# Double steps in the attention and feed-forward turns of a decoder block: two score tiles an instruction, whole outputs

## What is computed

```
x = x + attn(layernorm(x))                       # 16 heads, not touched
# cross-attention: q = layernorm(x), k = v = ctx; rows are split in 8 heads of 64 rows
qk  = einsum('bhdq,bhdl->bhql', qh, kh) / sqrt(64)
ret = einsum('bhql,bhdl->bhdq', softmax(qk), vh)
x = x + gamma * ret
# feed-forward, hidden size 1365, ternary weights w1q, w3q, w2q
g = silu(layernorm(x) @ w1q.T) * (layernorm(x) @ w3q.T)
x = x + g @ w2q.T
```

## Time and profile before

| | us |
|---|---|
| median of three runs | 1113.23 (1113.21 to 1115.01) |
| profiled execution | 1114.2 |
| its span, first to last instruction | 1112.1 |
| PE, DVE, ACT, POOL busy | 1104.1, 731.4, 550.5, 483.9 |
| turn (1, 0) | about 723 to 831 |
| turn (2, 1) | about 831.7 to 939 |
| turn (3, 2) | about 939 to 1047 |
| last turn, with the output's write | about 1047 to 1112 |

### The profile page before, as it was taken

The page is one execution under the profiler, slowest core; times in us unless marked ns, Lnnn a source line. Parts: engine busy times, 40 slices in busy tenths (PEclk is TensorE's granted clock), DMA queues, the critical chain, the costliest instruction groups (busy, mean ns, idle before and its releaser), DMA issues.

```text
span 1112.1 us, 15909 instructions
## 1 busy us (share of the span) xinstructions
PE 1104.1 (99%) x5840; PEld 938.7 (84%) x5840; DVE 731.4 (66%) x1347; ACT 550.5 (50%) x1149; POOL 483.9 (44%) x430
## 2 busy tenths in 40 slices
PE   9999999999999999999999999999999999999998
PEld 8888888878888888888888888888888888888886
DVE  7555547787777688866424334689967976887531
ACT  4556673324243376667515233167627763775130
POOL 1322327341424275665344040157728762875130
PEclk9999999999999999999999999999999999999999
DMA  7455553544533724212631112362113211310101
GB/s 246 164 189 189 185 176 129 171 126 159 173 111 93 230 96 142 86 39 86 252 114 38 38 59 65 140 205 63 53 52 101 77 49 58 113 49 1 38 1 38
DMA packets 54663, 122.20 MB, mean 110 GB/s; under 512 B 10057, under 2 KB 10057, under 8 KB 52538
## 3 DMA queue, kind: packets, MB, share of 16 engines
q1 hardware_dynamic: 54586, 121.18, 33.3%
HBM read 103.32 MB, written 17.84 MB: 109 GB/s over the span
## 4 chain that ended last, share of the span: by engine, by line
PE 94%; DVE 2%; DMA 1%; ACT 1%; issue 1%; POOL 0%; SPq 0%; POOLq 0%; DVEq 0%
PE bank L176 19%; PE bank L178 19%; PE bank L177 19%; PE bank L583 7%; PE bank L584 7%; PE bank L541 5%; PE bank L599 4%; PE bank L598 4%; PE bank L565 3%; PE bank L566 3%; PE bank L551 2%; PE bank L552 2%; DMA x1d<-x_scratch 1%; PE bank L608 0%; DVE x3l L860 0%
## 5 line engine op out<-in xcount | busy, mean ns | idle before, releaser
L583 PE MATMUL bank<-x3h,w 128*128 128x512 f32 (+2 forms) x368 | 143.5, 393 | 0.4 <-DVE x3l L860 0.3
L1471 ACT ACTIVATE yh<-bank 128x512 fp32r<-128x512 f32 x64 | 38.1, 600 | 209.9 <-PE bank L178 209.8
L584 PE MATMUL bank<-x3l,w 128*128 128x512 f32 (+2 forms) x368 | 140.6, 385 | 0.0
L940 POOL TENSOR_SCALAR pe_x<-pe_x,xri,gam 128x512 f32<-128x512 f32 x96 | 76.2, 795 | 78.5 <-DVE xri L779 76.1
L775 DVE TENSOR_REDUCE xmx<-bank 128x1 f32<-128x512 f32 x128 | 87.7, 687 | 32.9 <-PE bank L552 31.4
L2143 POOL TENSOR_TENSOR wal<-raw_a,wah 128x512 fp32r<-128x512 f32 x44 | 61.0, 1413 | 109.5 <-ACT wah L1513 109.5
L176 PE MATMUL bank<-wah,gh 128*128 128x512 f32 x256 | 102.6, 401 | 0.0
L2148 POOL TENSOR_TENSOR wbl<-raw_b,wbh 128x512 fp32r<-128x512 f32 x64 | 87.0, 1383 | 34.1 <-ACT wbh L1534 33.8
L176 PE MATMUL bank<-yh,rh 128*128 128x512 f32 x256 | 100.4, 392 | 0.8 <-DVE xacc L1979 0.8
L176 PE MATMUL bank<-wah,ph 128*128 128x512 f32 x256 | 100.1, 391 | 0.0
L177 PE MATMUL bank<-wal,gh 128*128 128x512 f32 x256 | 100.1, 391 | 0.0
(11 more groups left out here) (181 smaller groups left out, 3014.7 us busy)
## 6 DMA issues: line engine op xcount, KB each, us to landing
raw_a<-in_wk SPq DMA_DIRECT2D x8, 1024.0 KB, 5.2
raw_b<-in_wq SPq DMA_DIRECT2D x8, 1024.0 KB, 5.6
raw_a<-in_wo SPq DMA_DIRECT2D x8, 1024.0 KB, 5.1
raw_b<-in_wvt SPq DMA_DIRECT2D x8, 1024.0 KB, 5.0
ternary_scratch<-wraw SPq DMA_DIRECT2D x24, 341.2 KB, 3.0
x1d<-x_scratch SPq DMA_DIRECT2D x48, 128.0 KB, 3.1
kd<-in_ctx SPq DMA_DIRECT2D x48, 128.0 KB, 3.0
w<-ternary_scratch SPq DMA_DIRECT2D x2, 2730.0 KB, 11.1
```

The lines of the kernel that those rows point to most:

```text
L583: pe.matmul(u_bank[w][0:m, cols], lhs, x3h[:, c, cols], start=c == 0, stop=False)
L584: mm = pe.matmul(u_bank[w][0:m, cols], lhs, x3l[:, c, cols], start=False, stop=c == CK - 1)
L940: pool.tensor_scalar(m.pe_x[:, q, :], m.pe_x[:, q, :], xri[:, q:q + 1], gam[:], ALU.mult, ALU.mult).then_inc(s["xpn"], 1)
```

## The change

A turn has 16 double steps (`STEPS`), each for two score tiles (h, q) and (h, q + 1) with q = 0 or 2.

- The first four banks are two PSUM tensors of two banks each, so that one instruction can read two tiles: maxima (`dve_max_two`), reciprocals, the high and low parts of the transposed shares (`act_px_two`, `dve_px_two`). Exponentials and shares stay one tile an instruction.
- PE makes two score tiles, then two transposed tiles, then in steps q = 0 a whole output with 512 columns (`pe_ret_whole`) of head h - 2, then one up piece, or two in the odd steps from 3 to 13.
- ACT, steps q = 0: both exponentials, then a wait for the output of head h - 2, then the high parts; steps q = 2: the high parts, then the exponentials. Keys and queries come behind the gate.
- DVE: maxima, reciprocals of the step before, an up product, the next head's queries, `dve_ret`, the low parts, a further up product.
- POOL: the next head's queries first, then shares, the up part, keys, values.
- The rest of head 7 stands otherwise between the down tiles; four matmuls of down tile 1 move ahead of the last output.
- `r_done` gives the count of the semaphore r_ready, as sequence 0 still makes halves.

```diff
-        bank = [stack.enter_context(nc.psum_tensor(f"bank{i}", [P, 512], F32)) for i in range(8)]
+        two = [stack.enter_context(nc.psum_tensor(f"two{i}", [P, 2, 512], F32)) for i in range(2)]
+        bank = [t[:, k] for t in two for k in range(2)]
+        bank += [stack.enter_context(nc.psum_tensor(f"bank{i}", [P, 512], F32))[:] for i in range(4, 8)]
...
+        STEPS = 2 * XH
...
-            if n < 0 or n >= S_TILES:
+            if n < 0 or n >= STEPS:
                 return range(0)
-            return range(U_PIECES * n // S_TILES, U_PIECES * (n + 1) // S_TILES)
+            first = n + max(0, min(n, STEPS - 2) // 2 - 1)
+            return range(first, first + (2 if n % 2 and 1 < n < STEPS - 1 else 1))
...
+        def pe_ret_whole(pe, m, b, h):
+            pe.wait_ge(s["t_free"], t_p(b, h, 3) + 1)
+            if h % 2 == 0:
+                pe.wait_ge(s["vtl"], b * V_TILES + h // 2 + 1)
+            pe_wait(pe, "r_free", b * XH + h, 1)
+            for c in range(CK):
+                lhs = m.vts[:, h % 4, c, :]
+                pe.matmul(m.r[:], lhs, m.pxh[:, c, :], start=c == 0, stop=False)
+                mm = pe.matmul(m.r[:], lhs, m.pxl[:, c, :], start=False, stop=c == CK - 1)
+            mm.then_inc(s["r_ready"], 1)
...
         def pe_turn(pe, b, f, nxt):
+            for n in range(STEPS):
+                h, q = n // 2, n % 2 * 2
+                if b is not None:
+                    for k in (q, q + 1):
+                        pe_sx(pe, main, b, h, k)
+                    if h:
+                        for k in (q, q + 1):
+                            pe_pt(pe, main, b, h - 1, k)
+                    if h >= 2 and q == 0:
+                        pe_ret_whole(pe, main, b, h - 2)
+                if f is not None:
+                    for piece in pieces(n):
+                        pe_up(pe, f, piece)
             if f is not None:
                 pe_down(pe, f, 0, range(0, HC // 2))
             if b is not None:
-                pe_pt(pe, main, b, XH - 1, 2)
+                pe_ret_whole(pe, main, b, XH - 2)
+                pe_pt(pe, main, b, XH - 1, 0)
+                pe_pt(pe, main, b, XH - 1, 1)
             if f is not None:
                 pe_down(pe, f, 0, range(HC // 2, HC))
             if b is not None:
+                pe_pt(pe, main, b, XH - 1, 2)
                 pe_pt(pe, main, b, XH - 1, 3)
-                pe_ret(pe, main, b, XH - 1, 0)
             if f is not None:
-                pe_down(pe, f, 1, range(0, 3))
+                pe_down(pe, f, 1, range(0, HC // 2))
             if b is not None:
-                pe_ret(pe, main, b, XH - 1, 1)
+                pe_ret_whole(pe, main, b, XH - 1)
             if f is not None:
-                pe_down(pe, f, 1, range(3, HC))
+                pe_down(pe, f, 1, range(HC // 2, HC))
...
+        def act_px_two(act, b, h, q):
+            tiles, high, _ = shares(h, q)
+            act.wait_ge(s["t_ready"], t_p(b, h, q + 1) + 1)
+            act.activation(high, tiles, ACT.Copy).then_inc(s["pxh"], 2)
...
         def act_turn(act, b, f, nxt):
+            for n in range(STEPS):
+                h, q = n // 2, n % 2 * 2
                 if f is not None:
+                    for piece in pieces(n - 1)[-1:]:
                         act_tanh(act, f, piece)
                 if b is not None:
+                    if h and q:
+                        act_px_two(act, b, h - 1, q)
+                    elif h:
+                        act.wait_ge(s["t_ready"], t_p(b, h - 1, q + 1) + 1)
                     act_exp(act, main, b, h, q)
+                if f is not None:
+                    for piece in pieces(n)[:-1]:
+                        act_tanh(act, f, piece)
+                if b is not None:
+                    act_exp(act, main, b, h, q + 1)
+                    if h >= 2 and q == 0:
+                        act.wait_ge(s["r_ready"], r_done(b, h - 2))
+                    if h and q == 0:
+                        act_px_two(act, b, h - 1, q)
+                if f is not None:
+                    for piece in pieces(n - 1):
+                        act_gate(act, f, piece)
+                if b is not None:
                     if prep_step(h) == n:
+                        act_prep(act, main, b, h + 1)
+                    if h % 2 == 0 and values_step(h) == n:
+                        act_vt(act, main, b, h)
...
+        def dve_px_two(dve, b, h, q):
+            tiles, high, low = shares(h, q)
+            dve.wait_ge(s["pxh"], b * S_TILES + (4 * h + q + 2))
+            dve.tensor_tensor(low, tiles, high.bitcast(F32), ALU.subtract).then_inc(s["t_free"], 2)
+
+        def dve_max_two(dve, b, h, q):
+            dve.wait_ge(s["s_ready"], b * S_TILES + (4 * h + q + 2))
+            dve.reduce_max(xmx[:, q:q + 2], two[0][:], axis=AX, negate=True).then_inc(s["xmx"], 2)
...
         def dve_turn(dve, b, f, nxt, between=None):
+            for n in range(STEPS):
+                h, q = n // 2, n % 2 * 2
                 if b is not None:
+                    dve_max_two(dve, b, h, q)
+                    if n:
+                        dve_rinv_two(dve, b, (n - 1) // 2, (n - 1) % 2 * 2)
                 if f is not None:
+                    for piece in pieces(n - 1)[-1:]:
                         dve_up(dve, f, piece)
                 if b is not None:
                     if prep_step(h) == n:
                         dve_q(dve, main, b, h + 1)
+                    if q == 0 and h >= 2:
+                        dve_ret(dve, main, b, h - 2)
+                    if h:
+                        dve_px_two(dve, b, h - 1, q)
+                if f is not None:
+                    for piece in pieces(n)[:-1]:
+                        dve_up(dve, f, piece)
...
         def pool_turn(pool, b, f, nxt):
+            for n in range(STEPS):
+                h, q = n // 2, n % 2 * 2
+                if b is not None and prep_step(h) == n - 1:
+                    pool_queries(pool, main, b, h + 1)
+                if b is not None and n:
+                    for k in range(2):
+                        pool_prob(pool, main, b, (n - 1) // 2, (n - 1) % 2 * 2 + k)
...
                 if b is not None:
+                    if prep_step(h) == n:
+                        pool_keys(pool, main, b, h + 1)
                     if n - 1 in map(values_step, range(0, XH, 2)):
+                        pool_vt(pool, main, b, h)
```

More of the change, by code:

```diff
@@ L48 @@
 assert WP * WS * GROUPS == HID * C
-TANH_LAG, GATE_LAG = 1, 1
 WARM = 34
@@ L693, in act_px, with shares @@
             act.activation(m.pxh[:, :, q * P:(q + 1) * P], tb, ACT.Copy).then_inc(s["pxh"], 1)
+        def shares(h, q):
+            cols = slice(q * P, (q + 2) * P)
+            return (two[1][:].rearrange("p k (c n) -> p k c n", n=P),
+                    pxh[:, :, cols].rearrange("p c (k n) -> p k c n", n=P),
+                    pxl[:, :, cols].rearrange("p c (k n) -> p k c n", n=P))
+        def act_px_two(act, b, h, q):
+            tiles, high, _ = shares(h, q)
+            act.wait_ge(s["t_ready"], t_p(b, h, q + 1) + 1)
+            act.activation(high, tiles, ACT.Copy).then_inc(s["pxh"], 2)
         def act_exp(act, m, b, h, q):
@@ L730, in act_turn @@
                     act_exp(act, main, b, h, q)
-                    if prep_step(h) == n:
[L732 to L739, removed]
@@ new lines, in act_turn @@
+                if f is not None:
+                    for piece in pieces(n - 1):
+                        act_gate(act, f, piece)
+                if b is not None:
+                    if prep_step(h) == n:
+                        act_prep(act, main, b, h + 1)
+                    if h % 2 == 0 and values_step(h) == n:
+                        act_vt(act, main, b, h)
+            if f is not None:
+                for piece in pieces(STEPS - 1)[-1:]:
+                    act_tanh(act, f, piece)
+                for piece in pieces(STEPS - 1):
+                    act_gate(act, f, piece)
@@ L746, in act_turn @@
             if b is not None:
-                for q in range(4):
-                    act_px(act, main, b, XH - 1, q)
+                for q in (0, 2):
+                    act_px_two(act, b, XH - 1, q)
                 if nxt is not None:
@@ L870, in dve_turn @@
                 if f is not None:
-                    for piece in pieces(n - TANH_LAG):
+                    for piece in pieces(n - 1)[-1:]:
                         dve_up(dve, f, piece)
                 if b is not None:
-                    if h:
-                        dve_px(dve, main, b, h - 1, q)
-                    if n:
-                        dve_rinv(dve, main, b, (n - 1) // 4, (n - 1) % 4)
                     if prep_step(h) == n:
                         dve_q(dve, main, b, h + 1)
-                    if q == 3 and h >= 4 and h % 2 == 0:
+                    if q == 0 and h >= 2:
+                        dve_ret(dve, main, b, h - 2)
@@ L881, in dve_turn @@
+                    if h:
```

(18 more changed lines are left out.)

80 lines of the change are left out of this document (26 added, 54 removed).

## The result

The changed kernel takes 1135.3 us (1135.2 to 1135.6) against 1113.3 us for the kernel before, four runs of each: a ratio of 1.0195, 95% interval 1.0182 to 1.0207. It is slower, as forecast, but by 22 us where 11 were forecast, and above the upper end of the range, 1130. In the profiled executions the span grows by 21.3 us (1133.4 against 1112.1).

A forecast was written before the change was run, and what follows sets the result against it. The prediction took TensorE, without slack, as the bound. Its terms, -1.35 + 3.6 + 8.9 - 0.8 + 0.6 + 0.2, gave +11 us on the median of 1113.2, a forecast of 1124.2 us, range 1117 to 1130.

The forecast's parts named there:

- The bound: Whole kernel: TensorE waits for nobody, so only fewer or cheaper PE instructions or new PE holes move the time.
- Fewer PE instructions: Outputs of 8 matmuls instead of 16 and transposes eight in a row: PE gains 1.35 us.
- The double instruction: Cost of one two-tile instruction: 1.22 us on VectorE, 1.03 us on ScalarE.
- The start of a turn: First pairs of each of three turns: PE 1.42 and 1.54 us late, 2.96 a turn, 8.9 us in all.
- The steady wait: Transposes in odd steps from the third head on wait 0.2 us for dve_px_two: 3.6 us, from 0 to 7.
- The turn's end: Last output waits for the last dve_px_two: 0.2 us in each of three turns, 0.6 us, from 0 to 1.5.
- the last turn: Turn without attention: later gates hold gl2 back, 0.2 us (0 to 0.5).
- The stall at 748 us: First turn: PE's 0.78 us wait behind head 3's late load goes, since PE runs later: -0.8 us.
- Free moves: Reordered maxima, up products, rinv, keys, queries and pool work: hidden behind other work, no cost counted.
- Rival 2: Steady step: ScalarE binds, scores wait 0.5 us in 18 odd steps, +9 more, 1133 us; chance 0.06.
- Rival 3: Double instructions nearly as short as singles, 0.8 us instead of 1.22: 1114.2 us, no change; chance 0.09.
- rivals 1 and 4: Rival 1: only the turns' starts cost, 1120.7 us, chance 0.12. Rival 4: gaps close, faster, 1109.8 us, chance 0.07.

The follow-up runs named there:

- e10: Changed kernel with single instructions, turn (1,0)'s statistics every fourth double step, first head's high parts ahead of exponentials, last turn's gate ahead of the next tanh: 1115.8 us.
- e5: Changed kernel with the statistics of turn (1,0) eight at a time at the end of every fourth double step: 1131.5 us.

## Why the prediction was right in direction and short by half

**The bound.** Right: PE had no slack, and every added wait showed in the time.

**Fewer PE instructions, -1.35 us.** About right: where the waits are gone (e10), turns (2,1) and (3,2) are 0.43 and 0.39 us shorter than before; 0.45 a turn was worked out.

**The double instruction.** Right, 1.22 and 1.03 us.

**The start of a turn, 2.96 us.** Right: 0.84 + 0.61 + 1.76 = 3.2 us. Some 0.4 in the first matmuls behind these waits come on top, and the 0.4 that the kernel before lost there too goes off. Forecast as 1.42 and 1.54.

**The steady wait, 0.2 us in each of 18 odd steps.** Right in place and near in size: 0.24 to 0.33.

**The turn's end, 0.2 us, and the last turn, 0.2 us.** Under-sized: 0.46 and 0.53. The end (0.3 more than worked out), the steady waits (0.4 more) and the start (0.2 more) make about the 0.85 by which turns (2,1) and (3,2) exceed 3.9.

**The stall at 748 us.** Right: no wait for a load is left there in the kernel after. e10 shows that it is covered by the delay alone: with PE on time it comes back, as 1.7 us.

**Free moves.** This is the step that failed: "VectorE waits for the scores at 1.13 with the previous step's work done; up products follow at 2.4, and the bank they free is wanted 0.4 us or more later in the tightest step". It was worked out on turn (2,1) and taken for all three, as the start of turn (1,0) was, "with the same work behind it". In turn (1,0) the previous step's work ends with statistics that the sum nowhere names, a term put at nothing without a reason; two of them, moved together to where gtl and kl run, took 1.6 us instead of 0.33. The cover of 0.4 us could not hold that, and 7 us (120.09 against e5's 113.10) followed. Which turn a budget is made for matters: the earlier trace rows is the turn without `between`.

**The rivals.** Rival 2 named 1133 us, near the result, but not its mechanism: no scores wait for the second exponential in odd to even steps, and its deciding value, 1.6 us for a 1024 copy, measured 1.03. Rival 3 fell with 1.22, rivals 1 and 4 with the steady waits and the starts. A pair did save engine time (1.22 us against twice 0.69), but as the text beside rival 4 expected it bought nothing on PE. The rule of the Trainium skill named there ("VectorE: DVE Perf Modes", section on the TRN2 errata) is stated for operands in SBUF, while the double instructions here read PSUM, the low parts alone with one operand in SBUF.

## What to carry to other kernels

Pairing tiles in one instruction saves some time on its engine, which pays only where that engine is the bound. Here it was not: the pair's first tile was released late, and TensorE, which was fed without slack, paid the difference at each hand-over (4.75 us a turn, with VectorE idle for over 20). Before a reordering, make the budget for each variant of the loop body, the one with side work first, and look at the same form's mean in different stretches: 162 against 391 ns for one 128x4 instruction said that its place sets its price.

## What the runs showed of the hardware

A VectorE instruction on a 128x4 tile took 0.16 us alone and 1.16 to 1.21 us when issued just behind the start of a 1.28 us GpSimd instruction, and ended 0.02 to 0.03 us after it. The maximum from PSUM (1.23 us at 751.02) kept its usual length beside GpSimd's 1.29 us at 751.06.

The Trainium skill ("SBUF — State Buffer", section "Who interferes with whom") says that a VectorE instruction with two SBUF inputs, or one in a mode that uses both ports, can't share its second port pair with a GpSimd instruction that reads SBUF, that whichever was first holds it to its end, and that `tensor_reduce` never contends on trn2. The rows above agree in the first two points, with GpSimd first each time, and the maximum agrees with the third, though it reads PSUM, so its row says nothing of a reduction from SBUF. The price of a very small instruction, over seven times its own length, is theirs.
